# First attention of a four-layer kernel: the place of the first queries in ScalarE's order, and of a batch's addition and statistics in VectorE's

## The chip, the cores and the metric

The kernel runs on one core of one Trainium2 chip (trn2). The metric is device time in microseconds. Times of one execution under the profiler are read beside the median of several timed runs. Engines: TensorE (PE; its weight loads are shown apart as PEld), VectorE (DVE), ScalarE (ACT), GpSimd (POOL) and SyncE (SP), which issues the DMAs.

## What is computed

Four layers on x of 16 x 256 x 128 numbers in fp32. Each layer is `x += ga * attention(layernorm(x) * (1 + ca) + sa)` and then `x += gb * ffn(...)` with gates from a small conditioning product. The first layer's attention, which the change touches, has 64 query heads over 8 key/value heads of width 64, a sliding window of 128, and a learned sink:

```python
q = (x @ Wq.T + bq);  k = (x @ Wk.T + bk);  v = (x @ Wv.T + bv)      # 64, 8 and 8 heads of 64
scores = einsum('bhqd,bhkd->bhqk', q, k) / sqrt(64)
scores = where((qi >= kj) & (qi - kj < 128), scores, -1e30)
probs  = softmax(concat([scores, sink], -1))[..., :-1]
out    = einsum('bhqk,bhkd->bhqd', probs, v) @ Wo.T + bo             # 4096 -> 128
```

Behind it stand a mixture of experts, a latent attention, a soft mixture, a linear recurrence, a second mixture, a third attention and a last mixture. The change leaves them alone.

## The kernel before, in words

**Groups and cycles.** The first attention works in 128 groups: 16 batches (256 rows each) times 8 groups of 8 query heads, which share one key/value head. A group `n` has two units, `2n` and `2n + 1`, of four heads each. The stage is a pipeline of cycles (`attention_rounds`): cycle `n` makes the scores of group `n`, turns (transposes) the probabilities of group `n - 1` ("turning"), and multiplies the values and the output weights of group `n - 2` ("leaving"). It also projects queries for group `n + 1` ("ahead"), and either keys for two groups ahead (`n` even) or values (`n` odd), called `kv`. Each engine has its own list of steps, in an order written out by hand; engines meet only at semaphores.

**TensorE** (`attention_pe`) runs in a cycle: scores of the even unit (L497), values of the leaving group (L537), scores of the odd unit (L497), turn of the even unit of the turning group (8 transposes, L176), first queries `q0` ahead (L473), output product of the leaving group (`out`, 8 matmuls, L521), `kv` (keys L464 or values L468), turn of the odd unit (L176), second queries `q1` ahead (L473). The four projections all write one PSUM bank, `side`. So each waits on the semaphore `free` until the one before has been emptied: `kv` waits for ScalarE's two activations that empty `q0` (L729), and `q1` waits for VectorE's emptying of `kv`.

**ScalarE** (`attention_act`) holds: `weights` (L736), an exponential of 128 x 128 scores with a sum, eight for each unit; `outputs` (L749), which copies the summed values of one unit to SBUF; `turned` (L743), which copies half of the turned probabilities; `project` (L729), which empties the first queries; `sinks` (L760), small. Both `outputs` of a group wait for the same count of `values`. `begin` is waits alone.

**VectorE** (`attention_dve`): for each unit `masks` (two merges L631, eight masked maxima L643) and `shift` (L663); `inverse` (L670); `parted` (L653, two predicated copies of the other half of the turned probabilities); the emptying of `q1` (L611), of keys (L615) and of values (L622). In the last cycle of a batch it also forms the gated output (L705), which TensorE turns back into rows (L176, two transposes in the bank `acc`, semaphore `yread`). VectorE then adds these to the rows of x (L713, semaphore `x`) and takes the statistics of the batch's two tiles for the next layer norm (`stats`, L185 and L187). TensorE's scores wait for the masks of the unit before (semaphore `masked`), since there are three score banks. TensorE's first output product of the next batch waits for `x`, for it overwrites `acc`.

**GpSimd** (`attention_pool`) adds sinks (L815, L826) and multiplies the probabilities by the inverse sums (L830), unit after unit. **SyncE** issues no DMA within the stage; the next load waits for all 32 statistics.

Of the kernel before, what the change touches and what calls it, by code (L numbers as in the profile page):

```python
# [12 lines left out]
ALU = mybir.AluOpType  # L13
# [3 lines left out]
NB = 16  # L17
# [57 lines left out]
def past(e, sig, v):  # L75

    if v > 0:
        e.wait_ge(sig.sem, sig.base + v)


def done(inst, sig, when=True):
    if when:
        inst.then_inc(sig.sem, 1)
# [95 lines left out]
def stats(k, e, i):  # L179

    n = k.n_stats
    k.n_stats += 1
    st = k.st6[:, 6 * (n % 4):6 * (n % 4) + 6]
    past(e, k.s_aggr, n - 3)
    k.cd.then(e.bn_stats(st, k.X[:, i * 128:(i + 1) * 128]))  # L185
    k.cd.hold(e)
    e.bn_aggr(k.MV[:, 2 * i:2 * i + 2], st).then_inc(k.s_aggr.sem, 1)  # L187
# [255 lines left out]
def attention_rounds(a):  # L443


    for n in range(a.groups + 2):
        group = lambda lag: n - lag if 0 <= n - lag < a.groups else None
        ahead = n + 1 if n + 1 < a.groups else None
        yield group(0), group(1), group(2), ahead, attention_side(a, n)
# [138 lines left out]
def attention_dve(k, a, e):  # L588
    s, w, c_ = a.s, a.w, k.cd
# [14 lines left out]
    def project(step, n):  # L604
        g = n % a.nG
        e.wait_ge(*s["side"](a.uses[step, n] + 1))
        if step != "v":
            past(e, s["half"], 12 * (n - 1) if step == "q1" else 12 * (n - 2))
        if step == "q1":
            for c in range(2):  # L610
                done(e.tensor_scalar(a.qT[n % 2][:, 512 + 256 * c:768 + 256 * c], a.side[:, 256 * c:256 * c + 256],  # L611
                                     w["bq"][:, 4 * g + 2 + c:4 * g + 3 + c], None, ALU.add), s["free"], c == 1)
        elif step == "k":
            kt = a.kT[n // 2 % 2]
            e.tensor_scalar(kt[:, 0:256], a.side[:, 0:256], a.bk[:, g // 2:g // 2 + 1], None,  # L615
                            ALU.add).then_inc(s["free"].sem, 1)
        else:

            m = n // 2
            past(e, s["values"], 8 * (m + 1 - a.nv))  # L620
            bv = w["bv"][:, 64 * g:64 * g + 128].unsqueeze(1).broadcast_to([P, 2, 128])
            e.tensor_tensor(a.va[m % a.nv].rearrange("p (t w) -> p t w", t=2),  # L622
                            a.side[:, 0:256].rearrange("p (t w) -> p t w", t=2), bv, ALU.add).then_inc(s["free"].sem, 1)
# [9 lines left out]
    def mask(i, bank):  # L633

        sm, mx = a.Sm[i % 2], a.mxs[i % 4]
        e.wait_ge(*(s["half"](6 * i + 6) if bank == 2 else s["merged"](2 * i + 2 - bank)))
        for x in range(4 if bank == 2 else 2):
            if bank == 2:
                at, src, m, col = 512 + 128 * x, a.Sb[2][:, 128 * x:128 * x + 128], a.turnedmask if x % 2 else k.C["mwin"][:, 128:256], x
            else:  # L640
                h = 2 * bank + x
                at, src, m, col = 128 * h, a.Sb[bank][:, 256 * x:256 * x + 128], k.C["mcaus"][:, 0:128], 4 + h
            done(e.tensor_tensor_reduce(sm[:, at:at + 128], src, m, 1.0, -3.0e38, ALU.add, ALU.max, mx[:, col:col + 1]),  # L643
                 s["masked"], x == (3 if bank == 2 else 1))
# [12 lines left out]
    def shift(i):  # L657
        ng = a.ngs[i % 4]
        q0 = 8 * (i // 2 % a.nG) + 4 * (i % 2)
        over = lambda ap: ap[:, q0:q0 + 4].unsqueeze(1).broadcast_to([P, 2, 4])  # L660
        e.wait_ge(*s["masked"](3 * i + 3))
        past(e, s["exps"], i - 3)
        e.scalar_tensor_tensor(out=both(ng), in0=both(a.mxs[i % 4]), scalar=-a.scale, in1=over(a.nsink), op0=ALU.mult,  # L663
                               op1=ALU.min).then_inc(s["shift"].sem, 1)
# [7 lines left out]
    def masks(i):  # L672
# [5 lines left out]
        mask(i, 2)  # L678
        mask(i, 0)

    e.memset(a.Sb[2][:, :], 0.0).then_inc(s["part"].sem, 1)
    project("k", 0)
    project("v", 0)
    for n, turning, leaving, ahead, kv in attention_rounds(a):
        if n is not None:
            project("q1", n)
            masks(2 * n)
            shift(2 * n)
        if turning is not None:
            inverse(2 * turning + 1)  # L690
        if n is not None:
            masks(2 * n + 1)
        if turning is not None:
            parted(2 * turning)
        if n is not None:
            shift(2 * n + 1)
        if kv is not None:
            project(*kv)
        last = leaving is not None and leaving % a.nG == a.nG - 1
        b = leaving // a.nG if last else 0  # L700
        if last:
            ga = k.modT[:, 96 * a.l + 32 + b:96 * a.l + 33 + b]
            e.wait_ge(*s["out"](leaving + 1))
            past(e, s["yread"], b)
            e.tensor_scalar(a.yT, a.acc[:, 0:256], w["bo"], ga, ALU.add, ALU.mult).then_inc(s["y"].sem, 1)  # L705
        if turning is not None:
            parted(2 * turning + 1)
        if n is not None:
            inverse(2 * n)
        if last:  # L710
            x = k.X[:, 256 * b:256 * b + 256]
            e.wait_ge(*s["yread"](b + 1))
            e.tensor_tensor(x, x, a.acc[:, 0:256], ALU.add).then_inc(s["x"].sem, 1)  # L713
            e.wait_ge(*s["x"](b + 1))
            stats(k, e, 2 * b)
            stats(k, e, 2 * b + 1)


def attention_act(k, a, e):
    s, w = a.s, a.w  # L720
    e.wait_ge(*k.s_h(16 * a.no + 16))
    e.wait_ge(*a.t_w)

    def project(n):
        g = n % a.nG
        e.wait_ge(*s["side"](a.uses["q0", n] + 1))
        past(e, s["half"], 12 * (n - 1))
        for c in range(2):
            done(e.activation(a.qT[n % 2][:, 256 * c:256 * c + 256], a.side[:, 256 * c:256 * c + 256], ACT.Identity,  # L729
                              bias=w["bq"][:, 4 * g + c:4 * g + c + 1], scale=1.0), s["free"], c == 1)  # L730

    def weights(i, first, last):
        for x in range(first, last):
            c = 4 + x if x < 4 else x - 4
            at, w_ = 128 * x, 128
            done(e.activation(a.Pr[i % 4][:, at:at + w_], a.Sm[i % 2][:, at:at + w_], ACT.Exp,  # L736
                              bias=a.ngs[i % 4][:, c:c + 1], scale=a.scale,
                              accum_out=a.dens[i % 4][:, c:c + 1]), s["exps"], x == 7)

    def turned(i):  # L740
        e.wait_ge(*s["turn"](2 * i + 2))
        past(e, s["values"], 4 * (i // 2))
        e.activation(a.PT[i % 2][:, 0:512], a.Tb[i % 2][1][:, :], ACT.Copy, bias=0.0, scale=1.0).then_inc(s["even"].sem, 1)  # L743

    def outputs(v):
        m, s4 = divmod(v, 2)
        e.wait_ge(*s["values"](4 * m + 4))
        past(e, s["out"], m - 1)
        e.activation(a.oT[m % 2].rearrange("p (s a t q) -> p s t a q", s=2, a=2, t=2)[:, s4],  # L749
                     a.Ob[v % 2][:, :].rearrange("p (t a q) -> p t a q", t=2, a=2), ACT.Copy, bias=0.0,  # L750
                     scale=1.0).then_inc(s["o"].sem, 1)

    def begin(x):
        e.wait_ge(*s["shift"](x + 1))
        past(e, s["turn"], 2 * (x - 3))
        past(e, s["inv"], x - 3)

    def sinks(x):
        e.wait_ge(*s["sshift"](x + 1))
        e.activation(a.ess[x % 4], a.tks[x % 4], ACT.Exp, bias=0.0, scale=1.0).then_inc(s["sexp"].sem, 1)  # L760

    project(0)
    for n, turning, leaving, ahead, kv in attention_rounds(a):
        if turning is not None:
            weights(2 * turning + 1, 2, 8)
            sinks(2 * turning + 1)
        if leaving is not None:
            outputs(2 * leaving)
        if n is not None:
            begin(2 * n)  # L770
            weights(2 * n, 0, 3)
        if leaving is not None:
            outputs(2 * leaving + 1)
        if n is not None:
            weights(2 * n, 3, 6)
        if turning is not None:
            turned(2 * turning)
        if ahead is not None:
            project(ahead)
        if n is not None:  # L780
            weights(2 * n, 6, 8)
            sinks(2 * n)
            begin(2 * n + 1)
            weights(2 * n + 1, 0, 2)
        if turning is not None:
            turned(2 * turning + 1)
# [2528 lines left out]
```

## Time and profile before

| | us |
| --- | --- |
| median of three timed runs | 3936.39 |
| lowest, highest of the three | 3925.64, 3940.66 |
| profiled execution, its own time | 3932.3 |
| profiled execution, span | 3930.5 |
| first attention (74 to 1437 in the profile, without its first cycles) | 1363 |

Busy shares of the span: TensorE 91%, its weight loads 63%, VectorE 78%, ScalarE 57%, GpSimd 37%. Busy time says how long instructions lay on an engine, not what sets the end. For that the page has a chain followed back from the last instruction: here 54% TensorE, 18% VectorE, 15% ScalarE, 9% issue. Ends of matmuls are modelled and overlap the next start, so distances on TensorE are best taken from start to start.

### The profile page before, as it was taken

Reading aid. Unit: us, or ns where it says so; the run is one execution under the profiler, and the core shown is the slowest. Engines: PE = TensorE matmul, PEld = TensorE weight load, DVE = VectorE, ACT = ScalarE, POOL = GpSimd, SP = SyncE. Lnnn points to the kernel's source line nnn. Section 1 sums busy time; section 2 is a strip of 40 time slices with the busy share of each in tenths; the row PEclk is TensorE's granted clock in tenths of the full one; section 3 lists DMA queues with packets and bytes.
Section 4 is the critical chain, followed back from the end, with each engine's and each line's share of the span. In section 5 each row is a group of like instructions: output and inputs, shape, how many; then the busy total and the mean of one; then the engine's idle time right before and its main releaser. Section 6 shows DMA issues by size and latency. Waiting matters only on the chain.

```text
span 3930.5 us, 93870 instructions
## 1 busy us (share of the span) xinstructions
PE 3571.8 (91%) x32894; PEld 2460.4 (63%) x32894; DVE 3064.1 (78%) x11272; ACT 2233.5 (57%) x6991; POOL 1442.7 (37%) x1741
## 2 busy tenths in 40 slices
PE   7999999999999989989989978989887999899955
PEld 5888888888888875666644433335555666555532
DVE  6888888888888866767769976776885777788771
ACT  5888888888888862247754434433433222377611
POOL 2444444444444430035538856540100000222117
PEclk8999999999999989969989989999997999899958
DMA  3000000000000002310000000000000000000023
GB/s 128 3 3 3 3 3 3 3 3 3 3 3 3 3 30 82 88 71 2 2 1 0 0 11 1 1 1 1 1 1 33 1 1 1 5 30 2 23 59 48
DMA packets 30897, 64.58 MB, mean 16 GB/s; under 512 B 3424, under 2 KB 19808, under 8 KB 29152
## 3 DMA queue, kind: packets, MB, share of 16 engines
q1 hardware_dynamic: 24288, 52.29, 3.8%
q0 software_dynamic: 6144, 6.30, 1.0%
q8 instruction: 266, 4.36, 0.5%
q14 instruction: 199, 1.63, 0.1%
HBM read 49.93 MB, written 8.65 MB: 15 GB/s over the span
## 4 chain that ended last, share of the span: by engine, by line
PE 54%; DVE 18%; ACT 15%; issue 9%; POOL 2%; DMA 1%; DVEq 0%; ACTq 0%; POOLq 0%; SPq 0%
PE ps L537 7%; PE ps L176 5%; PE ps L497 4%; ACT W L736 4%; PE ps L473 3%; PE ps L1677 3%; PE ps L1648 3%; PE ps L1646 3%; ACT T L736 3%; PE ps L2301 2%; PE ps L2288 2%; DVE gbbc L2340 2%; ACT T L729 2%; PE ps L1017 2%; DVE gbbc L2329 2%
## 5 line engine op out<-in xcount | busy, mean ns | idle before, releaser
L736 ACT ACTIVATE T<-T 128x128 f32<-128x128 f32 x1024 | 397.8, 394 | 18.9 <-DVE T L663 18.9
L736 ACT ACTIVATE W<-T 128x128 f32<-128x128 f32 x1024 | 397.8, 394 | 4.5 <-DVE T L663 4.5
L643 DVE CUSTOM_DVE_ANT_0 T<-ps,C 128x128 f32<-128x128 f32 x1536 | 380.7, 285 | 0.0
L653 DVE COPY_PREDICATED W<-gbbc,ps 128x512 f32<-128x512 int32 x512 | 342.2, 721 | 3.8 <-PE ps L176 3.2
L497 PE MATMUL ps<-T 64*64 64x192 f32 (+2 forms) x8192 | 319.0, 292 | 16.8 <-DVE T L643 16.8
L537 PE MATMUL ps<-W,gbbc 64*64 64x128 f32 (+1 forms) x6912 | 319.8, 310 | 2.4 <-DVE W L653 2.4
L497 PEld LDWEIGHTS ps<-T 64*64 64x64 f32 x8192 | 257.6, 134 | 95.9 <-issue 60.9
L176 PE MATMUL ps<-C,T 128*128 128x128 f32 (+1 forms) x1620 | 263.2, 300 | 49.2 <-DVE T L307 18.9
L830 POOL TENSOR_TENSOR W<-W,T 128x512 f32<-128x512 f32 x256 | 260.8, 1040 | 122.8 <-DVE T L670 122.8
L830 POOL TENSOR_TENSOR T<-T 128x512 f32<-128x512 f32 x256 | 260.8, 1040 | 115.5 <-DVE T L670 115.5
L1244 POOL TENSOR_TENSOR QK<-T,QK 128x512 fp32r<-128x512 f32 x128 | 162.7, 1281 | 377.7 <-ACT T L1204 259.3
L537 PEld LDWEIGHTS ps<-W,gbbc 64*64 64x64 f32 x6912 | 280.2, 132 | 28.6 <-PE ps L537 23.2
L1183 ACT ACTIVATE T<-ps 128x384 f32<-128x384 f32 (+1 forms) x512 | 236.0, 550 | 69.8 <-PE ps L968 69.8
L473 PE MATMUL ps<-HT,W 128*128 128x256 f32 x1024 | 266.7, 383 | 2.2 <-ACT HT L334 1.1
L176 PEld LDWEIGHTS ps<-C,T 128*128 128x128 f32 (+1 forms) x1620 | 194.1, 148 | 102.5 <-issue 21.6
L749 ACT ACTIVATE T<-ps 128x512 f32<-128x512 f32 x256 | 150.2, 588 | 185.0 <-PE ps L537 185.0
L521 PE MATMUL ps<-T,W 128*128 128x256 f32 x1024 | 242.1, 379 | 1.8 <-ACT T L749 1.8
L1698 ACT ACTIVATE T<-ps,W 128x512 f32<-128x512 f32 x128 | 87.8, 687 | 240.1 <-PE ps L1646 240.1
L521 PEld LDWEIGHTS ps<-T,W 128*128 128x128 f32 x1024 | 194.3, 190 | 28.5 <-issue 2.2
L631 DVE COPY_PREDICATED ps<-C,ps 128x256 f32<-128x256 int32 x512 | 201.3, 427 | 11.5 <-PE ps L497 3.9
L176 PE MATMUL ps<-C,W 128*128 128x128 f32 x1202 | 168.4, 282 | 33.6 <-DMA W<-hrow_dram,T 14.2
L736 ACT ACTIVATION_READ_ACCUMULATOR W<-T 128x1 f32 x1024 | 198.5, 194 | 0.0
(420 smaller groups left out, 8838.9 us busy)
## 6 DMA issues: line engine op xcount, KB each, us to landing
T<-crow_dram SPq DMA_DIRECT2D x128, 128.0 KB, 3.0
W<-in_l1f_dram SPq DMA_DIRECT2D x1, 6152.0 KB, 18.1
W<-in_l0a_dram SPq DMA_DIRECT2D x1, 5172.5 KB, 25.3
W<-in_l2f_dram SPq DMA_DIRECT2D x1, 3160.0 KB, 10.7
W<-in_l3f_dram SPq DMA_DIRECT2D x1, 3076.0 KB, 10.2
W<-in_sm_dram SPq DMA_DIRECT2D x1, 2729.0 KB, 9.0
W<-in_l0f_dram SPq DMA_DIRECT2D x1, 2256.0 KB, 30.2
X<-in_x_dram SPq DMA_DIRECT2D x1, 2048.0 KB, 7.7
```

What stands on the lines that cost most here:

```text
L176: return e.transpose(out, in_, k.C["ident"])
L473: done(e.matmul(a.side[:, 256 * c:256 * c + 256], w["wq"][:, 512 * g + 128 * (2 * j + c):512 * g + 128 * (2 * j + c) + 128], x, start=True ...
L497: m = e.matmul(o[64 * x:64 * x + 64, k1:k2], q[r, 256 * c + 128 * qt + 64 * y:256 * c + 128 * qt + 64 * y + 64], kt[r, k0 + k1:k0 + k2], s ...
L521: done(e.matmul(a.acc[:, 0:256], w["wo"][:, (g * a.CH + c) * 128:(g * a.CH + c + 1) * 128], a.oT[n % 2][:, 256 * c:256 * c + 256], start=( ...
L537: m = e.matmul(o, v[rows, 128 * tile + g0:128 * tile + g0 + 64], x, start=first and q == qs[0], stop=last)
L631: e.copy_predicated(tiles[:, 0], old.bitcast(I32), tiles[:, 1]).then_inc(s["merged"].sem, 1)
L643: done(e.tensor_tensor_reduce(sm[:, at:at + 128], src, m, 1.0, -3.0e38, ALU.add, ALU.max, mx[:, col:col + 1]), s["masked"], x == (3 if ban ...
L653: e.copy_predicated(a.PT[t % 2][:, 512 + 512 * j:1024 + 512 * j].rearrange("p (h w) -> p h w", h=4), is_.unsqueeze(1).broadcast_to([P, 4, ...
L736: done(e.activation(a.Pr[i % 4][:, at:at + w_], a.Sm[i % 2][:, at:at + w_], ACT.Exp, bias=a.ngs[i % 4][:, c:c + 1], scale=a.scale, accum_o ...
L830: e.tensor_tensor(pr, pr, a.rins[i % 4][:, c:c + 4].unsqueeze(2).broadcast_to([P, 4, 128]), ALU.mult).then_inc(s["norm"].sem, 1)
L1183: e.activation(a.PT[n % 2][:, 512 * g:512 * g + 256 + a.w1], a.far[g][:, 0:256 + a.w1], ACT.Exp, bias=0.0, scale=a.scale).then_inc(s["exp" ...
L1244: e.tensor_tensor(dst, a.whole[m % 2], dst.bitcast(F32), ALU.subtract).then_inc(s["low"].sem, 1)
```

## The change

On ScalarE, the second `outputs` of the leaving group moves up behind the first; the emptying of the first queries (`project(ahead)`) stands behind four exponentials of the even unit, and not behind six and the first `turned`; `turned` comes behind it, with four exponentials after it.

On VectorE, the addition to the rows moves out of the batch's last cycle into the next cycle, between `shift(2n)` and `inverse` of the turning group. The statistics of the two tiles, both taken at the end of the batch's last cycle before, are now taken one at the end of each of the next two cycles. For the last batch all of it follows the loop. The gated output L705 stays where it was. Line numbers from L681 on move.

```diff
@@ attention_dve
+    def add(b):
+        x = k.X[:, 256 * b:256 * b + 256]
+        e.wait_ge(*s["yread"](b + 1))
+        e.tensor_tensor(x, x, a.acc[:, 0:256], ALU.add).then_inc(s["x"].sem, 1)
+        e.wait_ge(*s["x"](b + 1))
+
...
             project("q1", n)
             masks(2 * n)
             shift(2 * n)
+        if leaving is not None and leaving >= a.nG and leaving % a.nG == 0:
+            add(leaving // a.nG - 1)
         if turning is not None:
             inverse(2 * turning + 1)
...
         if n is not None:
             inverse(2 * n)
-        if last:
-            x = k.X[:, 256 * b:256 * b + 256]
-            e.wait_ge(*s["yread"](b + 1))
-            e.tensor_tensor(x, x, a.acc[:, 0:256], ALU.add).then_inc(s["x"].sem, 1)
-            e.wait_ge(*s["x"](b + 1))
-            stats(k, e, 2 * b)
-            stats(k, e, 2 * b + 1)
+        if leaving is not None and leaving >= a.nG and leaving % a.nG < 2:
+            stats(k, e, 2 * (leaving // a.nG - 1) + leaving % a.nG)
+    add(NB - 1)
+    stats(k, e, 2 * NB - 2)
+    stats(k, e, 2 * NB - 1)
...
@@ attention_act
         if leaving is not None:
             outputs(2 * leaving)
+            outputs(2 * leaving + 1)
         if n is not None:
             begin(2 * n)
-            weights(2 * n, 0, 3)
-        if leaving is not None:
-            outputs(2 * leaving + 1)
-        if n is not None:
-            weights(2 * n, 3, 6)
+            weights(2 * n, 0, 4)
+        if ahead is not None:
+            project(ahead)
         if turning is not None:
             turned(2 * turning)
-        if ahead is not None:
-            project(ahead)
         if n is not None:
-            weights(2 * n, 6, 8)
+            weights(2 * n, 4, 8)
             sinks(2 * n)
```

## Rows read from the trace of the kernel before

**Rows 1.** Part 1 of the page: busy time, share of the span, instructions.

```profile
PE 3571.8 (91%) x32894; PEld 2460.4 (63%) x32894; DVE 3064.1 (78%) x11272; ACT 2233.5 (57%) x6991; POOL 1442.7 (37%) x1741
```

**Rows 2.** Stretch: us, busy PE, PEld, DVE, ACT, POOL (counts), granted clock, DMA.

```profile
74.00:1437.00 1363.00, 1333.97 (x19304) 1127.75 (x19302) 1169.36 (x5991) 1163.25 (x5037) 659.02 (x1133) 1.00 0.01 3
```

**Rows 3.** Chain that ended last, in an ordinary cycle: start us, us, what.

```profile
605.10 0.73 ACT T L729 x2
...
605.87 0.71 PE ps L468 x4
```

**Rows 4.** Waits, 50 to 1440 us: total us, times, longest us.

```profile
PEld ps L468 <- ACT T L729: 33.7, 63, 1.3
...
PE ps L497 <- DVE T L643: 14.8, 16, 2.0
```

**Rows 5.** TensorE's timeline (start, us, instruction [idle before]): ordinary, batch-end, next cycle.

```profile
602.99 1.03 PE L473 MATMUL ps<-HT,W 128*128 128x256 f32 x4
...
603.86 1.89 PE L521 MATMUL ps<-T,W 128*128 128x256 f32 x8
...
606.42 1.04 PE L176 MATMUL ps<-C,T 128*128 128x128 f32 x8
...
607.29 1.03 PE L473 MATMUL ps<-HT,W 128*128 128x256 f32 x4
...
609.32 2.50 PE L537 MATMUL ps<-W,gbbc 64*64 64x256 f32 x54
...
611.59 0.73 PE L497 MATMUL ps<-T 64*64 64x192 f32 x16
...
673.54 2.50 PE L537 MATMUL ps<-W,gbbc 64*64 64x256 f32 x54
...
676.89 1.24 PE L497 MATMUL ps<-T 64*64 64x64 f32 x32 [0.86 <-DVE T L643]
...
679.86 1.89 PE L521 MATMUL ps<-T,W 128*128 128x256 f32 x8
...
682.10 1.04 PE L176 MATMUL ps<-C,W 128*128 128x128 f32 x8
```

**Rows 6.** Timeline of ScalarE, the same ordinary cycle.

```profile
601.24 0.60 ACT L749 ACTIVATE T<-ps 128x512 f32<-128x512 f32 x1 [1.42 <-PE ps L537]
...
601.73 0.39 ACT L736 ACTIVATE W<-T 128x128 f32<-128x128 f32 x1
...
604.52 0.58 ACT L743 ACTIVATE W<-ps 128x512 f32<-128x512 f32 x1
...
604.99 0.82 ACT L729 ACTIVATE T<-ps,W 128x256 f32<-128x256 f32 x2
...
606.48 0.21 ACT L760 ACTIVATE T<-T 128x8 f32<-128x8 f32 x1
```

**Rows 7.** Timeline of VectorE: ordinary cycle, batch's end, the cycle behind it.

```profile
601.81 0.20 DVE L670 RECIPROCAL T<-T 128x8 f32<-128x8 f32 x1 [0.53 <-POOL T L826]
...
606.62 0.42 DVE L622 TENSOR_TENSOR gbbc<-ps,W 128x256 f32<-128x256 f32 x1 [0.93 <-PE ps L468]
...
608.40 0.84 DVE L611 TENSOR_SCALAR T<-ps,W 128x256 f32<-128x256 f32 x2
...
672.74 0.36 DVE L713 TENSOR_TENSOR X<-X,ps 128x256 f32<-128x256 f32 x1
...
673.14 0.29 DVE L185 BATCH_NORM_STATS2 st<-X 128x6 f32<-128x128 f32 x1
...
673.47 0.18 DVE L187 BATCH_NORM_AGGREGATE MV<-st 128x2 f32<-128x6 f32 x1
...
673.57 0.26 DVE L185 BATCH_NORM_STATS2 st<-X 128x6 f32<-128x128 f32 x1
...
673.96 0.86 DVE L611 TENSOR_SCALAR T<-ps,W 128x256 f32<-128x256 f32 x2
...
682.30 0.48 DVE L615 TENSOR_SCALAR T<-ps,T 128x256 f32<-128x256 f32 x1 [0.59 <-PE ps L464]
```

## Prediction

> **What bounds the kernel now.** I read the page first, then the stretch table, the waits, the chain, and last the timelines of single engines over one ordinary cycle and over one where a batch ends. The page puts TensorE at 91% of the span [rows 1]. In the first attention (74 to 1437 us) it is busy 1334 of 1363 us at a granted clock of 1.00, its 2.4 GHz level [rows 2]. That looks like a plain TensorE bound, but a modelled end hides short holes, so the chain decides: it does not stay on TensorE. In each cycle it leaves TensorE when the values are done (601.2), runs over ScalarE until the queries' second copy (L729), and returns to TensorE at L468 or L464 [rows 3]. The waits name this hand-over: 63 waits of L468's weight loads for L729, 0.5 us each, and as many of L464's, which the row shown stands for [rows 4]. The other row there is L497 waiting for VectorE's L643, 16 times, nearly all at batch ends [rows 4].
>
> **The ordinary cycle.** What does that wait cost TensorE? Eight 256-column matmuls take 1.89 us and four take 1.03 [rows 5], so one more costs 0.215 us; eight 128-column ones take 606.42 to 607.29, 0.109 each. From the first output matmul (603.86) to the second turn (606.42) pass 2.56 us; the twelve matmuls in it need 8 x 0.215 + 4 x 0.109 = 2.16. So 0.39 to 0.40 us are lost: a hole of 0.29 (605.58, where the next could start, to 605.87 [rows 3]), and 0.10 for a weight load that nothing covers. In the cycle behind a batch's end, where ScalarE is early against TensorE, the same stretch (8 + 2 matmuls of 256 columns, 2.15 needed) takes 679.86 to 682.10 = 2.24: only 0.09 lost [rows 5]. That cycle is the change's experiment made by the kernel itself: with the queries emptied in time nothing else shows up in the hole's place.
>
> **Part 1: ScalarE's order.** No instruction is added or removed. The side bank goes to keys or values only once L729 has emptied the first queries. Today L729 stands behind two outputs, six exponentials and a copy of turned weights; then behind two outputs and four exponentials. Step by step: the outputs start at 601.24 and the next instruction follows 0.49 later, and from 601.73 to 604.52 lie six exponentials and one output, so an exponential takes (2.79 - 0.49) / 6 = 0.385 [rows 6]. New: 601.24 + 2 x 0.49 + 4 x 0.385 = 603.76. There the queries are not ready: their matmuls (L473) run 602.99 to 604.02 [rows 5]. ScalarE waits 0.31 us, of which 0.05 is the hand-over (L729's end at 605.83 to L468 at 605.87 is 0.04 [rows 3]), starts at 604.07, and the pair takes 0.82 [rows 6]: free at 604.89 instead of 605.81. TensorE wants to load the next weights one matmul before 603.86 + 8 x 0.215 = 605.58, at 605.37. Slack about 0.4 us. So the whole 0.39 goes.
>
> Its cost elsewhere: (a) the second output moves ahead of three exponentials. Both outputs wait for the same count, and its reader L521 starts at 603.86, after it in either order. (b) The first turned copy goes from 604.52 to 604.79 or so, right behind the pair; its reader is the values of the next cycle at 609.32 [rows 5]. (c) The last exponential of the even half and its sink go from 606.48 to 606.80 [rows 6]; GpSimd adds, then VectorE's inverse follows at about 608.3, just ahead of 608.40 [rows 7]: 1 us of cover. (d) ScalarE's round: idle 1.42 us before the outputs [rows 6]. The cycle shrinks by 0.39 and the new wait takes 0.31; 0.7 us of idle remain. Behind the waiting L729 are queued the copy, 12 exponentials and two sinks, and all have this cover. If it were gone the price would be that wait, up to 0.31 a cycle, 124 x 0.31 = 38 us.
>
> Who is next late? VectorE idles 0.93 us before a values step (L622) and 0.59 before a keys step (L615) in the unhindered cycle [rows 7]. That cover shrinks with the hole, by 0.39 from 0.93, and the 0.59 was already measured without it. No stall. How many: keys or values are projected in 124 of the 126 cycles that also empty outputs; 15 of them follow a batch's end. 109 x 0.39 = 42.5, 15 x 0.08 = 1.2. **Gain 43.7 us.**
>
> **Part 2: the batch's addition and statistics.** Today a batch's last cycle ends with L713 and two pairs L185/L187: 672.74 to 673.96, 1.22 us ahead of the second queries L611 [rows 7]. The masks come late, and TensorE takes 673.54 to 676.89 = 3.35 us from the values' start to the next scores, against 609.32 to 611.59 = 2.27 [rows 5]. 1.08 us x 15 batches (the sixteenth ends the stage) = 16.2 us that would go if the work were free. The difference 1.22 - 1.08 = 0.14 is VectorE's margin in a batch's last cycle; in an ordinary one it is larger: L611 at 608.40 to L497 at 611.59 is 3.19, stalled 673.96 to 676.89 is 2.93, margin 0.26 [rows 5, 7].
>
> The addition goes ahead of L670 in the middle of a cycle: 0.40 us (672.74 to 673.14) into an idle time of 0.53 before L670 [rows 7]. It waits for the transposes of the cycle before, long done, and then for its own semaphore. Queued behind it are the inverse, and GpSimd's multiplication behind that. Bounds: nothing, or 15 x 0.40 = 6.0 if that idle were not usable; even then the 0.59 before the side step takes it up. I take nothing. TensorE's first output matmul of the next batch waits for the addition: it ends at 601.7 in the cycle's time, L521 starts at 603.86. Covered by 2 us.
>
> The statistics stay at the cycle's end, one pair in each of the next two cycles, just ahead of L611. One pair costs 0.43 (673.14 to 673.57) or 0.39 (673.57 to 673.96) [rows 7]. Against the margin of 0.26: 0.43 - 0.26 = 0.17 of stall, twice a batch, 30 x 0.17 = **5.1 us back**. Bounds: nothing (all hidden; adding work there cannot gain), and 15 x 0.82 = 12.3 (no margin). I take the value with the margin, since two rows of the same interval give it. No DMA, POOL or SP step is moved; the readers of the rows and of the statistics come after the stage, whose last two pairs stay last.
>
> The Trainium skill, page "VectorE: DVE Perf Modes", section "The DRAIN you can't avoid", says that the next operation does not start until the pipe is empty. By that rule a pair would cost its waits plus both full durations, about 0.51, and the stall would be 0.25 a time, 7.5 us in all, result 2.4 us later. The rows speak against it for independent neighbours: L187 lasts 0.18 and L185 starts 0.10 after it [rows 7]; the same page's section on two instructions with no wait between them allows that.
>
> **The sum.** 43.7 + 16.2 - 5.1 = 54.8 us. The profiled execution took 3932.3 us (span 3930.5), so 3877.5. It lies 4.1 below the median of the three timed runs (3936.39), which would give 3881.6. I say 3880.
>
> **Rivals.**
> A, the hole closes only in part. TensorE's queue takes the release later than 0.4 us after my reckoning, or the queries arrive later at ScalarE than their modelled end says. Against: in 15 cycles the hole is 0.09. For: slack is only 0.4 us. With half the gain: 3932.3 - 21.8 - 11.1 = 3899. Chance 0.10.
> B, the first part does nothing: ScalarE waits for the queries as long as it used to work, and frees them no sooner. For that L473 would have to come 0.9 us later than in the rows. Then only the batches gain: 3932.3 - 11.1 = 3921. Chance 0.04.
> C, slower: ScalarE's queue is blocked at its head. The wait for L473 stands in front of the turned copy and twelve exponentials. It is paid in full once it exceeds ScalarE's idle time of 1.42 us [rows 6]; I reckon 0.31. If the round turned into a chain (exponentials late, inverse late, multiplication late, first turn late, queries late, exponentials later still) and the wait grew to 1.58, each of 124 cycles would be 0.16 longer than today: 3932.3 + 20 = 3952. Against: the turn before L473 uses products that were ready before the cycle began. Chance 0.04. The Trainium skill states on the page "PSUM — Partial Sum Buffer", section "Engine vs sequencer instructions", that ScalarE's queue is strictly in order; nothing could pass the blocked copy.
> An all-hidden batch part (3872) and an all-paid one (3885) are inside my forecast.
>
> **How the numbers follow.** Forecast 0.82, A 0.10, B 0.04, C 0.04. Range: below, 3932.3 - 59.9 = 3872.4 with the statistics free, less the 6.7 by which the fastest run shown lies under the profiled one: 3866, rounded down to 3864. Above, 3884.7 with statistics paid in full, plus 8.4 for the slowest run: 3893, drawn out to 3902 to take in A. A change of 0.5% is 20 us, about what a measurement of this kernel can tell from none. Forecast and A are faster by more than that: 0.91 with B (0.4%) left as the same, 0.05, and slower 0.04.
>
> **What would show it.** In the profile after: the waits of L468 and L464 for ScalarE gone, and new ones of ScalarE's queries for L473, about 0.3 us x 124; ScalarE's idle before the outputs halved; ordinary cycles of 10.28 us; TensorE's L497 waiting for L643 about 30 times, 0.1 to 0.2 us each, instead of 15 times 0.86; the chain on TensorE throughout; the stage ending near 1382 instead of 1437. If cycles of 10.4 us or more remain, A holds; if the statistics' cycles are 0.4 longer than the others, the margin of 0.26 was wrong; if ScalarE idles nowhere, C.

## The result and the profile after

| | before | after |
| --- | --- | --- |
| timed runs, median (lowest to highest), us | 3936.54 (3925.64 to 3940.66) | 3865.85 (3861.37 to 3872.45) |
| profiled execution, its own time, us | 3932.3 | 3861.4 |
| span, us | 3930.5 | 3859.6 |
| first to last output product of the first attention, us | 1363.3 | 1307.2 |
| ordinary cycle of it, us | 10.67 | 10.28 |
| eight cycles of a batch, us | 86.35 | 82.70 |

The ratio is 0.9826, with an interval of 0.9800 to 0.9852: 70.7 us faster, where 56.5 were forecast. The time lies inside the range given, 14 us below the forecast. The lower half of the table says where to look: the attention gave 56.1 us, close to the 54.8 of the sum. The other 14.8 us between the two spans lie ahead of it and behind it, in code that the change does not touch.

The page of the kernel after, the head of its chain by engine, for the whole program (before, TensorE had 54%, ScalarE 15%):

```profile
PE 69%; DVE 17%; ACT 5%; issue 5%; POOL 2%; DMA 1%; DVEq 0%; POOLq 0%; ACTq 0%; SPq 0%
```

The chain in the attention, from 620 to 645 us, by line; it holds TensorE alone:

```profile
by line: PE ps L497 21.8%; PE ps L537 20.4%; PE ps L176 19.6%; PE ps L473 17.3%; PE ps L521 16.4%; PE ps L468 3.6%; PE ps L464 1.7%
```

Line numbers have moved: the first queries' emptying is now L735 (was L729), the outputs L755 (L749), the exponentials L742 (L736), the addition L684 (L713), the gated output L713 (L705). The waits of the kernel after from 50 to 1390 us (total us, times, longest us) answer to [rows 4]:

```profile
ACT T L755 <- PE ps L537: 112.0, 128, 3.2
...
ACT T L735 <- PE ps L473: 33.5, 127, 1.7
...
PE ps L497 <- DVE T L643: 2.2, 2, 2.0
...
PEld ps L464 <- ACT T L735: 1.3, 1, 1.3
PEld ps L468 <- ACT T L735: 1.3, 1, 1.3
```

Of the 63 waits of 0.5 us on each of the two weight loads one is left on each. The row of L497 has 2 waits where the prediction looked for some 30 of 0.1 to 0.2 us; they are there, but a stall of 0.13 us hides under the modelled end of the matmul before, as the next timeline shows. The wait has changed sides: ScalarE now stands 127 times, 0.26 us each, for the queries. It pays that from its own idle time before the outputs, which fell from 185.0 to 112.0 us.

TensorE's timeline, ordinary cycles and then those around a batch's end, answers to [rows 5]. The distance from one L521 row to the next is a cycle:

```profile
628.93 1.89 PE L521 MATMUL ps<-T,W 128*128 128x256 f32 x8
630.66 0.59 PE L464 MATMUL ps<-HT,W 128*128 128x256 f32 x2
...
639.20 1.89 PE L521 MATMUL ps<-T,W 128*128 128x256 f32 x8
640.93 0.61 PE L468 MATMUL ps<-W,HT 128*128 128x128 f32 x4
...
649.70 1.89 PE L521 MATMUL ps<-T,W 128*128 128x256 f32 x8
...
654.77 2.50 PE L537 MATMUL ps<-W,gbbc 64*64 64x256 f32 x54
657.14 1.24 PE L497 MATMUL ps<-T 64*64 64x64 f32 x32
...
660.10 1.89 PE L521 MATMUL ps<-T,W 128*128 128x256 f32 x8
...
670.53 1.89 PE L521 MATMUL ps<-T,W 128*128 128x256 f32 x8
```

L464 and L468 follow 1.73 us behind L521, eight steps of 0.216: no hole is left. The cycles are 10.27, 10.50 (the batch's end, with two more transposes), then 10.40 and 10.43 with the statistics. In the first of these two, the scores (L497) start 2.37 us behind the values (L537), where the unhindered distance is 2.27 [rows 5]: that is most of the small stall, which the list of waits does not show.

VectorE around the same batch's end answers to [rows 7]. The addition and the first statistics pair:

```profile
647.05 0.41 DVE L684 TENSOR_TENSOR X<-X,ps 128x256 f32<-128x256 f32 x1
647.66 0.20 DVE L670 RECIPROCAL T<-T 128x8 f32<-128x8 f32 x1 [0.19 <-DVE X L684]
...
652.06 0.48 DVE L615 TENSOR_SCALAR T<-ps,T 128x256 f32<-128x256 f32 x1 [0.52 <-PE ps L464]
...
653.74 0.18 DVE L670 RECIPROCAL T<-T 128x8 f32<-128x8 f32 x1
653.84 0.24 DVE L185 BATCH_NORM_STATS2 st<-X 128x6 f32<-128x128 f32 x1
654.11 0.18 DVE L187 BATCH_NORM_AGGREGATE MV<-st 128x2 f32<-128x6 f32 x1
654.21 0.86 DVE L611 TENSOR_SCALAR T<-ps,W 128x256 f32<-128x256 f32 x2
```

The addition lies in the idle time ahead of L670 that stood in the kernel before, and VectorE still idles 0.52 us before the keys. A statistics pair costs 653.84 to 654.21 = 0.37 us ahead of the second queries.

### The profile page after: what moved, and what is told of

The parts are those of the page before. It is cut to its first block, busy times and chain, and to the rows that moved or that the text cites. A ratio compares the mean times of both kernels' runs of the same rounds, so it can differ in the third digit from the quotient of the medians.

```text
span 3859.6 us, 93855 instructions
## 1 busy us (share of the span) xinstructions
PE 3530.1 (91%) x32894; PEld 2461.0 (64%) x32894; DVE 3056.9 (79%) x11272; ACT 2232.7 (58%) x6991; POOL 1442.2 (37%) x1741
## 4 chain that ended last, share of the span: by engine, by line
PE 69%; DVE 17%; ACT 5%; issue 5%; POOL 2%; DMA 1%; DVEq 0%; POOLq 0%; ACTq 0%; SPq 0%
PE ps L176 9%; PE ps L537 8%; PE ps L497 7%; PE ps L473 6%; PE ps L521 6%; PE ps L1680 3%; PE ps L1651 3%; PE ps L1649 3%; PE ps L2304 3%; PE ps L2291 2%; DVE gbbc L2343 2%; PE ps L1020 2%; DVE gbbc L2332 2%; DVE gbbc L2338 2%; PE ps L998 2%
## 5 line engine op out<-in xcount | busy, mean ns | idle before, releaser
L742 ACT ACTIVATE T<-T 128x128 f32<-128x128 f32 x1024 | 397.3, 399 | 9.0 <-DVE T L663 9.0
L742 ACT ACTIVATE W<-T 128x128 f32<-128x128 f32 x1024 | 397.1, 399 | 1.3 <-DVE T L663 1.3
L537 PE MATMUL ps<-W,gbbc 64*64 64x128 f32 (+1 forms) x6912 | 319.6, 310 | 2.1 <-DVE W L653 1.2
L497 PE MATMUL ps<-T 64*64 64x192 f32 (+2 forms) x8192 | 317.2, 292 | 4.2 <-DVE T L643 4.2
L497 PEld LDWEIGHTS ps<-T 64*64 64x64 f32 x8192 | 254.3, 133 | 83.3 <-issue 45.2
L537 PEld LDWEIGHTS ps<-W,gbbc 64*64 64x64 f32 x6912 | 280.1, 132 | 28.3 <-PE ps L537 23.1
L521 PE MATMUL ps<-T,W 128*128 128x256 f32 x1024 | 242.1, 379 | 1.3 <-ACT T L755 1.3
L521 PEld LDWEIGHTS ps<-T,W 128*128 128x128 f32 x1024 | 194.3, 190 | 27.9 <-issue 1.5
L755 ACT ACTIVATE T<-ps 128x512 f32<-128x512 f32 x256 | 139.0, 594 | 112.0 <-PE ps L537 112.0
L742 ACT ACTIVATION_READ_ACCUMULATOR T<-T 128x1 f32 x1024 | 203.7, 199 | 0.0
L742 ACT ACTIVATION_READ_ACCUMULATOR W<-T 128x1 f32 x1024 | 203.3, 198 | 0.0
```

The lines of the kernel that those rows point to most:

```text
L497: m = e.matmul(o[64 * x:64 * x + 64, k1:k2], q[r, 256 * c + 128 * qt + 64 * y:256 * c + 128 * qt + 64 * y + 64], kt[r, k0 + k1:k0 + k2], s ...
L521: done(e.matmul(a.acc[:, 0:256], w["wo"][:, (g * a.CH + c) * 128:(g * a.CH + c + 1) * 128], a.oT[n % 2][:, 256 * c:256 * c + 256], start=( ...
L537: m = e.matmul(o, v[rows, 128 * tile + g0:128 * tile + g0 + 64], x, start=first and q == qs[0], stop=last)
```

## Experiments

"Stage" below is the time from the first to the last output product of the first attention; "batch" is the median distance over eight cycles between batch ends.

| kernel | ordinary cycle | batch | stage | median of runs (number) |
| --- | --- | --- | --- | --- |
| before, profiled again | 10.67 | 86.37 | 1363.6 | 3926.35 (1) |
| act_only | 10.28 | 83.54 | 1319.5 | 3884.66 (4) |
| dve_only | 10.67 | 85.56 | 1351.6 | 3914.17 (10) |
| after, profiled again | 10.28 | 82.70 | 1307.2 | 3870.19 (4) |
| turned_only | 10.28 | 83.57 | 1320.4 | 3884.08 (1) |
| outs_only | 10.67 | 86.29 | 1362.2 | 3925.24 (1) |
| w7 | 10.57 | 84.79 | 1339.4 | 3903.57 (1) |
| stats_pair | 10.29 | 82.97 | 1311.1 | 3867.01 (1) |
| stats_mid | 10.28 | 82.43 | 1303.0 | 3866.11 (4) |
| pad15 | 10.28 | 82.70 | 1307.2 | 3883.14 (4) |
| after, a third profile | 10.28 | 82.69 | 1307.2 | 3875.70 (1) |

### Each half alone

act_only is the kernel before with ScalarE's part of the change; dve_only is the kernel before with VectorE's part.

> ScalarE's new order alone; VectorE's addition and statistics stay in the batch's last cycle. Theory (two independent holes): ordinary cycles of 10.28 us, no wait of the key and value weight loads for ScalarE, but the wait of the scores for VectorE at 15 batch ends stays, 1.08 us each, and is now paid in full: a batch takes 8 x 10.28 + 0.22 + 1.08 = 83.5 us against 86.35. That is 42 us of the stage, and some 46 in all with the start. Rival (the two parts are one loop, either alone does little): under 25 us.

> The moved addition and statistics alone; ScalarE's order is that of before. Ordinary cycles stay at 10.67 us. The stall of 1.08 us at a batch's end goes, but in the kernel before 0.3 us of it were already given back, since the next cycle's hole behind ScalarE was closed by it; and the two small stalls of the statistics vanish in the holes of 0.39. So a batch takes 8 x 10.67 + 0.22 = 85.6 us against 86.35, 0.8 x 15 = 12 us in all. Rival (each statistics pair stalls the scores and is paid): 7 to 8 us.

Waits in act_only, 50 to 1400 us:

```profile
ACT T L729 <- PE ps L473: 43.1, 127, 3.7
...
PE ps L497 <- DVE T L643: 14.9, 16, 2.0
...
PEld ps L464 <- ACT T L729: 1.7, 1, 1.7
PEld ps L468 <- ACT T L729: 1.6, 1, 1.6
```

Waits in dve_only, 50 to 1440 us:

```profile
PEld ps L468 <- ACT T L735: 32.1, 63, 1.6
PEld ps L464 <- ACT T L735: 32.1, 63, 1.6
...
PE ps L497 <- DVE T L643: 2.2, 2, 2.0
```

Each half removes its own wait and leaves the other's (in act_only the 14.9 us of L497, in dve_only the 32.1 us of each weight load). ScalarE's half takes 43.8 us off the stage (43.7 in the sum of the prediction) and the ratio of act_only is 0.9873 (0.9848 to 0.9897). VectorE's half takes 11.7 us (0.9971, 0.9953 to 0.9989). Together 55.5, and the whole change 56.1: they add up, within 0.6 us. dve_only shows why VectorE's half does not bring its 16 us: in the kernel before, a TensorE that is late at a batch's end finds ScalarE early, so that 0.3 us of each stall came back in the next cycle (10.35 us in place of 10.67), and in dve_only the statistics hide in the holes that are still there. Its batch is 85.56 us, as worked out before it ran.

### Which step of ScalarE's reorder does it

The change moves two steps. turned_only moves one, outs_only the other, each in the kernel before:

```diff
 # turned_only
             weights(2 * n, 3, 6)
-        if turning is not None:
-            turned(2 * turning)
         if ahead is not None:
             project(ahead)
+        if turning is not None:
+            turned(2 * turning)
 # outs_only
             outputs(2 * leaving)
+            outputs(2 * leaving + 1)
         if n is not None:
             begin(2 * n)
-            weights(2 * n, 0, 3)
-        if leaving is not None:
-            outputs(2 * leaving + 1)
-        if n is not None:
-            weights(2 * n, 3, 6)
+            weights(2 * n, 0, 6)
```

> The kernel before with one step moved: the first queries are emptied ahead of the first turned copy, behind six exponentials and both outputs in their old places. Slack theory (the release may be 0.4 us later than in the changed kernel): ScalarE comes to the queries at 604.52 of the cycle in the prediction instead of 603.76, frees them at 605.35, the next weight load can start at 605.40 against 605.37 without a wait, and 0.11 us of that is covered by the matmul stream. Ordinary cycles 10.28 us, batch 83.5. Rival (the gain needs the queries to be met as soon as they are ready): a part of the hole stays, cycles of 10.45 or more.

> The kernel before with only the second output moved up behind the first. The queries stand behind the same ScalarE work as before, so nothing changes: ordinary cycles 10.67 us, batch 86.35. Rival (the early outputs help TensorE's output product or the batch ends): less than 10.6 us, or a batch end that is more than 0.3 us shorter.

turned_only has the cycle of 10.28 us in full; outs_only has 10.67. A single copy of 0.47 us behind the queries and not ahead of them brings 42.9 of ScalarE's 43.8 us. (outs_only takes 1.1 us off the stage: the cycle behind a batch's end goes from 10.35 to 10.27.) ScalarE's timeline in turned_only, for the cycle whose output product starts at 605.91:

```profile
603.28 0.60 ACT L749 ACTIVATE T<-ps 128x512 f32<-128x512 f32 x1 [1.17 <-PE ps L537]
...
606.56 0.82 ACT L729 ACTIVATE T<-ps,W 128x256 f32<-128x256 f32 x2
```

and TensorE's:

```profile
605.91 1.89 PE L521 MATMUL ps<-T,W 128*128 128x256 f32 x8
607.63 0.61 PE L468 MATMUL ps<-W,HT 128*128 128x128 f32 x4
```

The queries are met 3.28 us behind the outputs, as reckoned (604.52 less 601.24). They are empty at 607.38, and L468 starts at its unhindered place, 1.72 behind L521. ScalarE no longer waits for the queries in an ordinary cycle, and it keeps 1.17 us of idle time where the changed kernel has 0.85. So the changed kernel's early place for the queries is not needed; what counts is a deadline.

### How late may the queries be emptied

w7 puts seven exponentials ahead of the queries in the changed kernel:

```diff
-            weights(2 * n, 0, 4)
+            weights(2 * n, 0, 7)
...
-            weights(2 * n, 4, 8)
+            weights(2 * n, 7, 8)
```

> The changed kernel with seven exponentials ahead of the first queries in place of four, the last after the turned copy. ScalarE comes to the queries 1.16 us later than in the changed kernel, after 0.31 of waiting: release 0.85 later, next weight load 0.41 late, 0.30 of it seen by TensorE (a load 0.50 late cost 0.39). Ordinary cycles 10.58 us, most of the first part's gain lost. Rival (the order of turned copy and queries matters, not the time): 10.28.

TensorE's timeline in w7:

```profile
624.66 1.89 PE L521 MATMUL ps<-T,W 128*128 128x256 f32 x8
626.57 0.70 PE L464 MATMUL ps<-HT,W 128*128 128x256 f32 x2
...
635.22 1.89 PE L521 MATMUL ps<-T,W 128*128 128x256 f32 x8
```

L464 comes 1.91 us behind L521, where 1.73 is unhindered, and the cycle is 10.56 us (10.58 reckoned). The slack of 0.4 us is real and is spent after it. Medians over the ordinary cycles of each trace, in us behind the first output matmul:

| kernel | queries empty | next weight load starts | cycle |
| --- | --- | --- | --- |
| after | 1.04 | 1.51 | 10.28 |
| turned_only | 1.47 | 1.52 | 10.28 |
| w7 | 1.86 | 1.92 | 10.57 |
| before | 1.96 | 2.01 | 10.67 |

A release 0.43 later costs nothing. Where the load is 0.40 and 0.50 late, the cycle is 0.29 and 0.39 longer: the lateness less 0.11 in both. Nothing was measured between a load 0.01 late and one 0.40 late.

### What a statistics pair costs, and where it is free

stats_pair puts both pairs at the end of the first cycle behind a batch. stats_mid puts each pair ahead of the keys or values:

```diff
 # stats_pair, at the cycle's end
-        if leaving is not None and leaving >= a.nG and leaving % a.nG < 2:
-            stats(k, e, 2 * (leaving // a.nG - 1) + leaving % a.nG)
+        if leaving is not None and leaving >= a.nG and leaving % a.nG == 0:
+            stats(k, e, 2 * (leaving // a.nG - 1))
+            stats(k, e, 2 * (leaving // a.nG - 1) + 1)
 # stats_mid: the two lines of the changed kernel, moved up
             shift(2 * n + 1)
+        if leaving is not None and leaving >= a.nG and leaving % a.nG < 2:
+            stats(k, e, 2 * (leaving // a.nG - 1) + leaving % a.nG)
         if kv is not None:
             project(*kv)
```

> The changed kernel with both statistics pairs at the end of the first cycle behind a batch, none in the second. Margin theory (VectorE is 0.30 us ahead of the scores there; the changed kernel lost 0.13 in each of two cycles by pairs of 0.43): 0.82 - 0.30 = 0.52 in one cycle, nothing in the other; a batch takes 82.96 us against 82.70. Rival (each pair costs a fixed 0.13 wherever it stands): 82.70.

> The changed kernel with each statistics pair moved from the cycle's end to the place ahead of the keys or values, where VectorE idles 0.48 to 0.52 us in the changed kernel; a pair takes 0.43. Idle theory: the two stalls of 0.13 a batch go, a batch takes 8 x 10.28 + 0.22 = 82.44 us against 82.70, the stage is 3.9 us shorter (1303.3 against 1307.2). Rival (the keys' or values' emptying is late by the wait that the pair needs): 82.6 or more. The total is not told apart from the changed kernel by the timed runs.

TensorE's timeline in stats_pair, behind a batch's end:

```profile
569.13 1.89 PE L521 MATMUL ps<-T,W 128*128 128x256 f32 x8
...
576.97 1.24 PE L497 MATMUL ps<-T 64*64 64x64 f32 x32 [0.27 <-DVE T L643]
...
579.93 1.89 PE L521 MATMUL ps<-T,W 128*128 128x256 f32 x8
```

One cycle is 10.80 us and the next one 10.29: the loss is 0.52 for two pairs at once against 2 x 0.13 for two apart. A fixed price for each is out; a margin that is used once in each cycle explains both. VectorE's timeline in stats_pair gives its size:

```profile
656.25 0.24 DVE L185 BATCH_NORM_STATS2 st<-X 128x6 f32<-128x128 f32 x1
...
657.01 0.86 DVE L611 TENSOR_SCALAR T<-ps,W 128x256 f32<-128x256 f32 x2
```

Two pairs take 0.76 us, one takes 0.37: 0.76 - 0.52 = 0.24 and 0.37 - 0.13 = 0.24. The margin is about 0.25, as the prediction had it (0.26), and not the 0.30 that I wrote for stats_pair, where I still priced a pair at 0.43.

VectorE's timeline in stats_mid:

```profile
651.15 0.28 DVE L185 BATCH_NORM_STATS2 st<-X 128x6 f32<-128x128 f32 x1
651.47 0.18 DVE L187 BATCH_NORM_AGGREGATE MV<-st 128x2 f32<-128x6 f32 x1
651.76 0.48 DVE L615 TENSOR_SCALAR T<-ps,T 128x256 f32<-128x256 f32 x1
```

The pair fills the idle time of 0.52 and L615 comes when its keys do. Both stalls are gone: batch 82.43, stage 1303.0, 4.2 us under the changed kernel. That is the shortest stage of all. It shows in the trace alone: the timed runs (3866.11 against 3865.85 and 3870.19) do not tell the two kernels apart.

### Where the other 14.8 us come from

> The kernel before once more, unchanged. It tells how far two profiled executions of one kernel lie apart. Theory S (the 4.3 us won before the first output product and the 10.5 us won behind the attention belong to the change): the first output product starts again near 75.1 us, the first stretch at 1.2 GHz lasts some 24 us, and the second attention (heads) is no shorter than 346 us. Theory V (they are variation from run to run): start and heads move by 4 to 10 us against the first profile of the same kernel.

> The changed kernel once more. Stage as in its first profile (first to last output product 1307 us). Theory S: first output product near 70.8 us, heads some 8 us shorter than in the kernel before. Theory V: these two move by 4 to 10 us, the stage by under 1.

> The changed kernel a third time, on the chip of the two others. Stage 1307.2 us; time behind the last output product 2481 to 2489 if VectorE's part has to do with it, anywhere in 2481 to 2493 if it is chance.

The first output product starts at 75.1 and 71.2 us in the two profiles of the kernel before, and at 70.8, 76.4 and 75.2 in the three of the changed one. The stages agree within 0.3 us in each pair. So the 4.3 us at the start are variation. What varies is TensorE's clock while the pipeline fills. The same stretch, 44 to 76 us, in the kernel before and in the one after (busy PE, PEld, DVE, ACT, POOL, then the granted clock):

```profile
44.00:76.00 32.00, 25.61 (x298) 20.38 (x293) 22.30 (x130) 19.27 (x89) 10.65 (x19) 0.68 0.01 2
```

```profile
44.00:76.00 32.00, 25.59 (x353) 20.83 (x349) 25.97 (x139) 23.14 (x106) 11.93 (x22) 0.89 0.01 2
```

TensorE is as busy in both, but at a mean of 0.68 it does 298 matmuls and at 0.89 it does 353. All thirteen profiles fit this, whatever the kernel. By the traces' records of the clock, TensorE spends 13.7 us of the first 80 at 1.2 GHz in four of them, and the first output product starts at 70.8 to 72.1; it spends 17 to 21 us in four others (72.4 to 73.6), and 24 to 31 us in the last five (75.1 to 76.7). The kernel before and the changed one are each found in the first and in the last group.

Behind the last output product the change executes nothing. The three profiles of the changed kernel, from there to the end:

```profile
1378.10:3859.60 2481.50, 2181.86 (x13208) 1288.01 (x13208) 1846.15 (x5050) 1038.20 (x1843) 770.16 (x581) 0.92 0.07 20
```

```profile
1383.60:3868.30 2484.70, 2183.99 (x13208) 1289.91 (x13208) 1845.48 (x5050) 1038.19 (x1843) 770.30 (x581) 0.92 0.07 20
```

```profile
1382.40:3873.90 2491.50, 2198.27 (x13208) 1299.90 (x13208) 1845.94 (x5050) 1038.50 (x1843) 770.05 (x581) 0.91 0.07 19
```

VectorE, ScalarE and GpSimd are equally busy in all three. TensorE's time and the length rise as the clock falls, over 10 us; the kernel before has 2492.0 and 2489.7. The clock's records have 392, 402 and 441 us at 1.2 GHz in the three, and 419 and 422 in the kernel before. So the first profile of the changed kernel was a lucky one in this part. The timed runs say the same of one kernel on one chip: the thirteen of the kernel before that were taken together run from 3922.2 us at a granted clock of 0.946 to 3941.4 at 0.940.

For a while the lengths looked as if VectorE's half had to do with them: 2487.6 to 2493.0 in five profiles without it, 2481.5 to 2488.7 in five with it. VectorE's program has 15 waits fewer in that half (2945 against 2960), so later instructions stand elsewhere. pad15 was meant to test that:

```diff
             e.tensor_scalar(a.yT, a.acc[:, 0:256], w["bo"], ga, ALU.add, ALU.mult).then_inc(s["y"].sem, 1)
+            if b < NB - 1:
+                e.wait_ge(*s["out"](leaving + 1))
```

> The changed kernel with one more wait of VectorE, on a count long reached, in each of 15 batch ends, so that VectorE's program has again as many wait instructions as before (2960). The time from the last output product to the end of the span was 2487.6 to 2493.0 us in five profiles without VectorE's part of the change, 2481.5 to 2488.7 in five with it. Theory L (the place of the later instructions in VectorE's program matters): about 2490. Theory C (chance, or another cause): about 2484. Stage 1307 us in both.

It ran 2493.6 us there, which would speak for the place of the code. But its trace counts 2945 waits, as that of the changed kernel does: the added wait repeats one that stands just above it, and the edit did not do what it was for. So the place of the code stays untested, and pad15 is in effect the changed kernel once more; its four runs have a median of 3883.1, 17 us over the first four of that kernel. The unpadded kernel on the same chip had 2491.5. These runs are enough against the pattern: the changed kernel covers 2481.5 to 2491.5 by itself, and stats_mid, which has VectorE's half too, has 2488.8.

The thirteen profiles have a mean of 2490.1 us without VectorE's half and 2487.1 with it. Thirteen values drawn at random into such groups lie that far apart in one case of six, so 3 us are no sign of a cause, but they do not exclude one. The length goes with the time at 1.2 GHz, though loosely (correlation 0.76). All runs taken together (25 of before, median 3930.9; 9 of after, median 3870.1) are 60.8 apart, 4.7 more than the stage's 56.1. These 4.7 us stay unplaced.

## Why the prediction was right, and where it was off

**The bound.** The chain was read rightly: it went from TensorE over ScalarE to the keys and values, and with the hand-over early it stays on TensorE in the ordinary cycles.

**ScalarE's part, 43.7 us.** 43.8 in act_only. The kernel's own unhindered cycle, which stood in [rows 5], had given the answer. The steps on the way held too: slack 0.4 (turned_only and w7 bracket it), ScalarE's new wait 0.31 (0.26 measured as idle time, 127 times), and its idle before the outputs from 1.42 to 0.7 (0.85 measured). The Trainium skill, page "PSUM — Partial Sum Buffer", section "Engine vs sequencer instructions", calls ScalarE's queue strictly first in, first out. The trace agrees, and it did no harm: the turned copy stands behind the waiting queries (629.13, then 629.86 in the changed kernel), and what stood behind the blocked step had the cover it needed. Rivals A, B and C are out: no load waits for ScalarE in an ordinary cycle, and none of them would give 10.28 us.

**VectorE's part, 11.1 us.** 12.3 (act_only's stage less that of the changed kernel). The work, if it were free, was taken as worth 16.2 us, and is worth 16.5 (act_only less stats_mid). The mis-sized term is the statistics, 5.1 us back where 4.2 were measured (stats_mid). The margin of 0.26 was right and the pair's price was not: 0.43 was taken from a pair that stood behind the addition; behind L670 it is 0.37. The Trainium skill's rule in "VectorE: DVE Perf Modes", section "The DRAIN you can't avoid", would have priced it at 0.51, by the prediction's estimate. The measurement went the other way: L187 lasts 0.18 us and L611 starts 0.10 behind it (654.11, 654.21). The addition cost nothing, as said: in stats_mid, which keeps it in its new place, the cycle that holds it is 10.27 us. The 0.3 us that the kernel before gave back after each stall were not named in the prediction, though it used the cycle in which they came back; they change the split between the halves, not the sum.

**The total.** 3880 against 3865.85. The weak step is the one from the sum to the total: one profiled execution and three runs were taken as the level, with 6.7 and 8.4 us of spread at either side, and 2.5 us were added in rounding. The whole sum was 1.3 us short. The rest lies outside the stage, and much of it is which way two small sets of runs fell: the first set of before lies 5.6 us above the median of all its runs, the first set of after 4.3 below. Without these 9.9 us the 70.7 are 60.8, of which 56.1 are shown in the stage. The time came within 2 us of the lower end of the range, and two of its four runs lie under that end, so that the range held was partly luck; the account of the stage was not.

## What to carry to other kernels

Where several steps share one buffer, each emptying of it has a deadline, set by the next user on the bounding engine. Reckon it from start-to-start distances, and move only the step that misses it: one copy of 0.47 us was worth 43 us here, and the rest of ScalarE's new order 0.9. Small extra work goes where its engine already waits for something else (stats_mid), not at the end of a list where it uses up the margin of the engine that follows. And look for the cycle in the trace that happens to run without the hole: it is the experiment.

## What was not expected of the hardware

A hole is dearer than it looks. Weight loads held up by 0.50 us cost TensorE 0.39 us. The hole between two matmuls is only 0.28 us (2.01 behind the first output matmul in place of 1.73), since the load would have lain under the last matmul; but another 0.10 is lost right behind it, where the four matmuls of L468 take 0.55 us to the next step (605.87 to 606.42) in place of 0.44. And one unchanged kernel's time outside the stage varied by 10 us, with 392 to 441 us of it at 1.2 GHz. That is more than twice what the last refinement of the stage (4.2 us) brings; differences of that size can be read in a stage's trace and not in the total.
